# A causal mask as rows of the contraction, residues on GpSimd, and a new order of steps, in a hybrid block

## What is computed

```python
qkv = x @ qkv_w.T + qkv_b                      # 16 heads of width 8
q = q * cos + rotate_half(q) * sin;  k = k * cos + rotate_half(k) * sin
scores = einsum('bhsd,bhtd->bhst', q, k) / sqrt(8)
scores = where(key position > query position, finfo.min, scores)
out = softmax(scores) @ v,  then @ proj_w.T + proj_b
```

## Time and profile before

| | us |
|---|---|
| median of 3 runs | 749.57 |
| lowest and highest | 744.65 and 756.94 |
| the profiled execution | 753.01 |
| its span in the trace | 750.9 |

### The profile page before, as it was taken

The page is one execution under the profiler, slowest core; times in us unless marked ns, Lnnn a source line. Parts: engine busy times, 40 slices in busy tenths (PEclk is TensorE's granted clock), DMA queues, the critical chain, the costliest instruction groups (busy, mean ns, idle before and its releaser), DMA issues.

```text
span 750.9 us, 17433 instructions
## 1 busy us (share of the span) xinstructions
PE 653.8 (87%) x6640; PEld 375.3 (50%) x6670; DVE 563.3 (75%) x1571; ACT 426.4 (57%) x900; POOL 187.8 (25%) x231
## 2 busy tenths in 40 slices
...
PEclk9689896599999999999999999999999999999985
...
GB/s 107 1 1 1 16 69 101 2 17 2 87 100 1 17 98 89 2 10 66 113 17 24 52 99 29 2 58 76 55 9 56 63 64 17 96 75 3 16 1 14
DMA packets 20934, 32.37 MB, mean 43 GB/s; under 512 B 3178, under 2 KB 18282, under 8 KB 18538
## 3 DMA queue, kind: packets, MB, share of 16 engines
...
...
## 4 chain that ended last, share of the span: by engine, by line
PE 55%; DVE 24%; issue 8%; ACT 7%; DMA 3%; POOL 2%; SPq 1%; DVEq 0%; ACTq 0%; POOLq 0%
PE ps L1066 8%; PE ps L1021 8%; PE ps L1051 8%; DVE mrow L1491 7%; PE ps L795 5%; PE ps L869 3%; DVE qkf L1460 3%; PE ps L896 3%; PE ps L1053 3%; DVE am L1335 3%; PE ps L1023 2%; PE ps L790 2%; PE ps L916 2%; ACT pT L762 2%; PE ps L905 2%
## 5 line engine op out<-in xcount | busy, mean ns | idle before, releaser
L1491 DVE TENSOR_REDUCE mrow<-ps 128x1 f32<-128x384 f32 (+3 forms) x352 | 221.4, 634 | 78.5 <-PE ps L1023 76.0
L762 ACT ACTIVATE pT<-ps 128x512 f32<-128x512 f32 (+1 forms) x352 | 186.9, 558 | 105.1 <-PE ps L1053 101.6
L1021 PE MATMUL ps<-ks,qs 72*128 72x512 bf16 (+3 forms) x512 | 140.0, 309 | 17.3 <-DVE mrow L1491 14.1
L1051 PE MATMUL ps<-qs,ks 75*128 75x256 bf16 (+3 forms) x512 | 131.5, 305 | 4.1 <-DMA qs<-mT 2.5
L1023 PE MATMUL ps<-cbf 128*128 128x128 bf16 x512 | 101.5, 224 | 0.0
L1066 PE MATMUL ps<-pT,va 128*32 128x512 f32 (+3 forms) x1024 | 96.1, 451 | 5.3 <-ACT pT L762 5.0
L1021 PEld LDWEIGHTS ps<-ks,qs 72*128 72x128 bf16 x512 | 50.3, 99 | 96.0 <-DVE mrow L1491 78.2
L1053 PE MATMUL ps<-cbf 128*128 128x128 bf16 x512 | 98.0, 221 | 0.0
L546 POOL TENSOR_TENSOR spread<-state,cst 128x144 f32<-128x144 f32 x112 | 47.5, 445 | 186.8 <-DVE state L1364 153.2
L1051 PEld LDWEIGHTS ps<-qs,ks 75*128 75x128 bf16 x512 | 50.5, 99 | 76.0 <-ACT pT L762 30.6
L534 POOL TENSOR_TENSOR xe<-lpart,hot 96x1024 bf16<-96x1024 bf16 x32 | 60.3, 1893 | 47.8 <-DVE lpart L1321 47.8
...
## 6 DMA issues: line engine op xcount, KB each, us to landing
...
qs<-mT SPq DMA_DIRECT2D x48, 8.0 KB
```

The source lines that it names most:

```text
L762: act.activation(pT[:, c0:c0 + m, P_OFF[kt]:P_OFF[kt] + width], ps[:, score_banks(b)[n % len(score_banks(b))], 0:m * width].rearrange("p ( ...
L1021: pe.matmul(o, qs[0:K_MAX, f % RING, h, qt * P:(qt + 1) * P], ks[0:K_MAX, f % RING, h, 0:width], start=True, stop=False, skip_group_check= ...
L1051: pe.matmul(o, ks[0:K_ALL, place, h, kt * P:(kt + 1) * P], qs[0:K_ALL, place, h, kt * P:T], start=True, stop=False, skip_group_check=True)
L1491: dve.tensor_reduce(mrow[:, qt, h0:h0 + m], ps[:, max_banks(b)[n % len(max_banks(b))], 0:m * width].rearrange("p (m k) -> p m k", k=width) ...
```

## The change

Both mask matmuls go. Instead `qs` and `ks` get 43 more rows (`MARKS`, rows 75 to 117), written once: the row of a key and that of a query hold powers of two whose products add up to a large negative number exactly where the key is later than the query in its tile. They are built from the identity and a triangle by six DVE instructions on 43 columns, turned by two PE transposes, copied by ACT, and spread by six DMAs to the three places of the ring. Each product of scores is split: the diagonal tile takes 118 rows (`K_DIAG`), the rest of the width 72 rows (maxima) or 75 (attention). Where the tile is the whole width, there is one matmul. As rows 72 to 74 of `ks` hold ones, the same rows of `qs` must be zero during the maxima, so SP writes zeros there for each half batch (24 KB, one DMA more among those that `stacked` counts; PE's maxima wait for them).

In batches 1 to 6 (`residues_aside`) the four subtractions of the parts per batch move from DVE to GpSimd, behind its three `rsqrt` steps. All five order strings are written anew: DVE has 24 steps fewer for `m` and one more for `x`, GpSimd 24 more for `m`; PE, ACT and SP one more for `x` each, the setting up of the marks. The strings are left out here, and so are the declarations of semaphores.

```diff
-N_STACK = 16 * (len(Q_COPIES) + len(K_COPIES))
+N_STACK = 16 * (len(Q_COPIES) + len(K_COPIES) + 1)
+MARKS = (P + 2) // 3
+K_DIAG = K_ALL + MARKS
+MARK = (2.0 ** -39, 2.0 ** 12, 2.0 ** 63)
...
+        marks_tok = pT[:, 2, 0:MARKS].bitcast(BF16).rearrange("p (s r) -> p s r", s=2)
+        marks = pT[0:MARKS, 3, 0:T].bitcast(BF16).rearrange("p (s t) -> p s t", s=2)
...
-        ones_in = sem("ones_in")
+        ones_in = [sem("ones_in%d" % place) for place in range(RING)]
...
+        after = cst[:, C_AFTER:C_AFTER + P]
...
-        future_qk = cbf[:, P:2 * P]
...
+        def residues_aside(b):
+            return 0 < b < B - 1
...
         def va_heads(b):
...
+        zeros = consts_bf[0:1, 2 * P:3 * P].unsqueeze(1).broadcast_to([PARTS, HH * C, P])
...
-                sp.dma_start(ks[K_MAX:K_ALL, place, :, :], ones[:, 0:HH, :]).then_inc(ones_in, 16)
+                sp.dma_start(ks[K_MAX:K_ALL, place, :, :], ones[:, 0:HH, :]).then_inc(ones_in[place], 16)
             def norm(b):
...
+                    sp.dma_start(qs[K_MAX:K_ALL, f % RING, :, :].rearrange("p h (c t) -> p (h c) t", t=P), zeros
+                                 ).then_inc(stacked[f % RING], 16)
             def maxima(b):
+                if b == 0:
+                    yield
+                    sp.wait_ge(marks_ready, 1)
+                    for place in range(RING):
+                        for side, dst in enumerate((qs, ks)):
+                            sp.dma_start(dst[K_ALL:K_DIAG, place, :, :],
+                                         marks[:, side, :].unsqueeze(1).broadcast_to([MARKS, HH, T])
+                                         ).then_inc(marks_in[place], 16)
                 for f in (2 * b, 2 * b + 1):
...
+                for side in range(2 if residues_aside(b) else 0):
+                    yield
+                    pool.wait_ge(part0, b * 2 + side + 1)
+                    pool.tensor_tensor(rope1[:, side, :], qkf[:, side, :], parts[:, 0, side, :], ALU.subtract).then_inc(res1, 1)
+                for side in range(2 if residues_aside(b) else 0):
+                    yield
+                    pool.wait_ge(part1, b * 2 + side + 1)
+                    pool.tensor_tensor(parts[:, 2, side, :], rope1[:, side, :], parts[:, 1, side, :],
+                                       ALU.subtract).then_inc(part2, 1)
             def maxima(b):
...
             def maxima(b):
+                if b == 0:
+                    yield
+                    act.wait_ge(marks_ps, 1)
+                    act.activation(marks.rearrange("p s (c t) -> p s c t", c=C),
+                                   ps[0:MARKS, BK_MAX, :].bitcast(BF16)[:, 0:2 * P].rearrange("p (s t) -> p s t", s=2)
+                                   .unsqueeze(2).broadcast_to([MARKS, 2, C, P]), ACT.Copy).then_inc(marks_ready, 1)
                 for f in (2 * b, 2 * b + 1):
...
+                        if n == 0 and b == 0:
+                            for place in range(RING):
+                                act.wait_ge(marks_in[place], 32)
...
             def maxima(b):
...
+                if b == 0:
+                    yield
+                    pe.wait_ge(masks_in, 16)
+                    pe.wait_ge(marks_step, 6)
+                    for side in range(2):
+                        mm = pe.transpose(ps[0:MARKS, BK_MAX, :].bitcast(BF16)[:, side * P:(side + 1) * P],
+                                          marks_tok[:, side, :], ident_bf)
+                    mm.then_inc(marks_ps, 1)
                 for f in (2 * b, 2 * b + 1):
                     for n, (qt, h0, m) in enumerate(MAX_GROUPS):
...
-                                pe.wait_ge(masks_in, 16)
+                                pe.wait_ge(marks_ready, 1)
+                            if f < RING:
+                                pe.wait_ge(marks_in[f], 32)
+                                pe.wait_ge(ones_in[f], 16)
...
                         for h in range(h0, h0 + m):
...
-                            pe.matmul(o, qs[0:K_MAX, f % RING, h, qt * P:(qt + 1) * P], ks[0:K_MAX, f % RING, h, 0:width],
-                                      start=True, stop=False, skip_group_check=True)
-                            mm = pe.matmul(o[:, qt * P:(qt + 1) * P], ident_bf, future_qk,
-                                           start=False, stop=True, skip_group_check=True)
+                            own_tile = slice(qt * P, (qt + 1) * P)
+                            if qt > 0:
+                                pe.matmul(o[:, 0:qt * P], qs[0:K_MAX, f % RING, h, own_tile],
+                                          ks[0:K_MAX, f % RING, h, 0:qt * P], start=True, stop=True, skip_group_check=True)
+                            mm = pe.matmul(o[:, own_tile], qs[0:K_DIAG, f % RING, h, own_tile],
+                                           ks[0:K_DIAG, f % RING, h, own_tile], start=True, stop=True, skip_group_check=True)
...
                     for i in range(m):
...
-                        pe.matmul(o, ks[0:K_ALL, place, h, kt * P:(kt + 1) * P], qs[0:K_ALL, place, h, kt * P:T],
-                                  start=True, stop=False, skip_group_check=True)
-                        mm = pe.matmul(o[:, 0:P], ident_bf, future_kq, start=False, stop=True, skip_group_check=True)
+                        own_tile = slice(kt * P, (kt + 1) * P)
+                        mm = pe.matmul(o[:, 0:P], ks[0:K_DIAG, place, h, own_tile], qs[0:K_DIAG, place, h, own_tile],
+                                       start=True, stop=True, skip_group_check=True)
+                        if kt + 1 < C:
+                            mm = pe.matmul(o[:, P:width], ks[0:K_ALL, place, h, own_tile], qs[0:K_ALL, place, h, (kt + 1) * P:T],
+                                           start=True, stop=True, skip_group_check=True)
...
                 def values(g, kt):
...
-                if b == 0:
-                    pe.wait_ge(masks_in, 16)
-                    pe.wait_ge(ones_in, 16 * RING)
...
-                for side in range(2):
+                for side in range(0 if residues_aside(b) else 2):
...
-                for side in range(2):
+                for side in range(0 if residues_aside(b) else 2):
...
             def maxima(b):
+                if b == 0:
+                    yield
+                    dve.wait_ge(consts_in, 16)
+                    for k in range(3):
+                        n = len(range(k, P, 3))
+                        for side, (table, mark) in enumerate(((ident, -MARK[2 - k]), (after, MARK[k]))):
+                            to, columns = marks_tok[:, side, 0:n], table[:, k:P:3]
+                            if k == 0:
+                                ins = dve.tensor_scalar(to, columns, mark, None, ALU.mult)
+                            else:
+                                dve.wait_ge(marks_step, 2 * k)
+                                ins = dve.scalar_tensor_tensor(to, columns, mark, to, ALU.mult, ALU.add)
+                            ins.then_inc(marks_step, 1)
...
                 for f in (2 * b, 2 * b + 1):
                     for n, (qt, h0, m) in enumerate(MAX_GROUPS):
```

More of the change, by code:

```diff
@@ L86 @@
 PE_ORDER = (
[L87 to L96, removed]
@@ L97 @@
[L97 to L99 removed]
+    "ssssssssssmsssssssssssssssssssmsxssssssmmsssssmsmssssmsmssssssssssssssmssmssmsssmsssssssssssssmxssxsxxmx"
+    "sxxsxsxsxsxxsxsxsxsssxssxmxssxssxssxmxssxssxssxaassxaasaxsxaxssxsmaxamxssxsxsaaxmxaaasxaaxmxsxaamxsaxasx"
@@ new lines @@
+    "maxaaxasaaaasxaasssxaaxamaxsaxssaxaxaamaxaaxaasxaasaaxsasxasxaaaxasasxsaxaaamxaaxsaxmsxasxasxsxamsxasxax"
+    "ssxamxsaxaasxssxaaxssxasxaasaxaaxaaxsxaaxasxsxaaasxmaaxmxsxaxaasaaxsxaaxaaxaaaaxasaxamaasxsaaxmxssxaxasx"
+    "aaaaxasaxsxasaxasaxsasaxsxaaxaamxaaxsaxmassxsaxssxmxsaxsxasxsxsaxssxsxssxaxssxaaaxsxaamaxaaxsaasxaaxasax"
+    "saxaasamxasamxaaaasasaaaaxmaaaasxmaxasxsaxaaxasaaxaxasxsaxaaaxasxsxamxsaaxmaaaxsamxaaxaasxsaaxsxasxsasxs"
+    "axssmxsaxsxasxaxsssxasxaaxassxsxaasxsaxsaxaasxaasxaaxssaxaaaxaasxamaxaxaamaaxsaxasxaaaxaaaxasxaaaxasxaam"
@@ new lines @@
+    "xaaaxssxmxsxsaaxaxsaaxsaxasxaxaasaxaaxsamxaaxassaxmaxsaxsmaxssxasxassxmaxssxaxasxasxsxaasxaaxaassxaasxsx"
+    "aaxssxsaxaaaasaxsaxassaxaamsxamxsaxaaxaaaxaaaxsaxasxaaaxmasxaaaaxaxaaaxsxasxaaxmxaaxssaxaasxaaaxsaaxsaxm"
+    "axmassxsaxmsxasxassxasxaxasasxsxaxasxsxmxssxssxaaaaxssaaxssxaaxssxsaaaxaasasaaxssxaaxamaaxmaaxaaxaaaxaax"
+    "axaaxmaaxmxaaaxaaxaaaxaxaaxaxamaaxmxaaxaaxaaxamaxxaxaxaxmxaxxaxxaxaxaaxaaxaxaaxaaxaxaaxaxaaaxaxaaxaaaxaa"
+    "aaaxxaaaaxaxaxaxxxaaxxaaxxxaaaxaaaaaxaxaxxxaxaaaxaxaaaxaaaxxxaxaaxaxaxaxxxaaaaxxaxaxaxaaaxaxxaxaaxxaaaaa"
@@ L100 @@
+    "xaaaxaaaaaaaaaaaaaaaaaaaaaaaaaaaaaaaaaaaaaaaaaaaaaaaa"
 )
 ACT_ORDER = (
[L102 to L105, removed]
@@ new lines @@
+    "maasaaaamasaaaaaxasssaasaaaaasassaasmassasssaassasaaaasaasaamaaasamxsssssasnsmsaamaaamaamaasaaaasamaaaxa"
+    "aassasasaaamasssasaassasaaasaasassamsaamaaaasaaamaasasxsmssssamsanasasaamaaaaasaaaaaaamaaasaxaasasaaaaas"
```

(8 more changed lines are left out.)

27 lines of the change are left out of this document (16 added, 11 removed).

## The result

| | before | after |
|---|---|---|
| median, us | 749.8 | 794.79 |
| lowest and highest | 744.65 and 756.94 | 790.1 and 796.36 |
| profiled execution and its span | 753.01, 750.9 | 795.49, 793.7 |

The ratio is 1.061 [1.054, 1.069]: the change is slower, and my range ended at 741. (Ratios leave out runs over 1.5% above their kernel's fastest, medians are over all runs, and the two differ where a kernel scatters, as e5, e7 and e12 do.)

A forecast was written before the change was run, and what follows sets the result against it. PE's work was taken to set the middle's pace, DVE close behind. Masks 34 + residues 5.4 - collisions 2.5 - path 1.2 - zeros 0.5 - setup 1 = 34 us; four fifths, 27, off 749.6 gave 722 us, range 703 to 741.

The forecast's parts named there:

- The marks' transfers: Six spreads of marks on SP, 2.1 MB, would move while its queue is idle: cost 0, if late up to 18 us.
- 34 us of the masks lie on the chain: PE gives up 56 us net of splits; 61% of the masks lie on the chain, so 34 us net come off it.
- I take four fifths: Discount on the summed 34 us, as another chain shows when the longest shortens: 27 us of gain.
- the maxima don't gain: Rival, 17%: reductions and their one bank set the maxima's pace, so removing their masks brings nothing; gain 14 us, 736 us.
- A new order brings its own gain: Rival, 13%: redrawn order strings fill PE's waits, so all 34 us and 10 more come: 44 us, 705 us.
- PE busy down by more than 50 us: Sign expected in the changed profile: PE's busy time falls by over 50 us with the mask matmuls gone.
- The distance of 59 ns: On PE, 128-column matmuls start 59 ns apart, so 1024 masks cost 60 us; more contraction rows should cost nothing.
- Residues: +5.4, -2.5, -1.2: Chain effect of moving 24 subtractions to GpSimd: 5.4 us gained on DVE, 2.5 lost to collisions, 1.2 on the maxima's path.
- the 8 us: DVE time taken for collisions with the residues moved to GpSimd, between estimates of 6 and 31 us.
- Zeros 0.5, setting up 1: Chain costs: 0.5 us for 16 DMAs of zeros on SP, 1 us for preparing the marks in the first scan.
- The clock falls: Rival, 6%: less dense PE drops to 1.2 GHz for 80 us after 170 us: 767 us; for part of it, 740.
- GpSimd holds the scan: Rival, 4%: in batches 1 to 6 residues waiting for ACT delay `spread_state` and PE's `across`; at 8 us a batch, 771 us.

The follow-up runs named there:

- e5: The kernel before with its 1024 mask matmuls left out and nothing in their place, old order, residues on DVE: 758.92 us, ratio 0.996 to before.
- e7: The change with cut marks transfers (masks off, residues on GpSimd), but in the five order strings of the kernel before: 747.82 us, ratio 0.991 to before.
- e12: e1 with every score product whole over 72 or 75 rows and no mask, marks and zeros still transferred: 748.37 us, ratio 0.981 to before.
- e1: The changed kernel with each of the six marks transfers cut into 32, 8 and 3 rows: 725.49 us, ratio 0.970 to before.
- e4: The kernel before with marks (cut transfers) for its mask matmuls, residues on DVE, old order plus the marks' step: 751.65 us, ratio 1.002 to before.
- e9: The kernel before, mask matmuls kept, with residues on GpSimd and the five new order strings: 748.58 us, ratio 0.997 to before.
- e6: The kernel before, masks and order kept, with the residues of batches 1 to 6 on GpSimd: 753.44 us, ratio 1.003 to before.
- e3: e1 with the residues of batches 1 to 6 back on DVE: 755.6 us, ratio 1.005 to before.
- e8: e1 with each half batch's zeros sent in 24 packets of 1 KB instead of 96 small ones: 728.67 us, ratio 0.971 to before.
- e11: e9 with the mask matmuls left out and nothing in their place, so no marks, zeros or splits: 741.25 us, ratio 0.985 to before.
- e13: e12 with all score products over 118 rows, the marks being zeros: 726.28 us, ratio 0.968 to before.

## Why the prediction was wrong

**The marks' transfers, the step that failed.** "the marks are ready when PE has passed 29 steps of the first scan by its new order string, so they move while the queue is idle; cost 0". Three things in it were wrong. They were ready (ACT's copy of them ends at 56.2 us), but SyncE wasn't free to issue them: from 11.6 us on it stood at the load of `x` for batch 2 and waited for batch 1's `x` to be read, until 80.6 us. The trace of before has the same wait: there the load is issued at 78.8 us, in 0.40 us. The rate was taken from stacks of 72 rows and 9.83 us for 1.2 MB; 2.1 MB in rows of 43 took 6 x 14.8 = 89 us. And what stands behind them in SyncE's string, the spills, was priced at nothing: the bound "up to 18 us" is that of late marks alone. The hole is 69 us (after against e1).

**The sum without it.** 27 us forecast; e1 gains 750.91 - 725.49 = 25.4 us against the before timed with it, and 725 lies in my range. The size was right, several of its reasons were not:

- *34 us of the masks lie on the chain.* As a share of the present chain it was read rightly, as a gain it was not: in the old order the time doesn't fall (e4, and e5 without any mask), in part, by the estimate above, as the clock falls. "I take four fifths" can't stand for that: what the next chain is depends on the order, not on a fraction. The rival that the maxima don't gain (17%, 736 us) had the right mechanism for the old order, as waits for reductions grew by 20 us, but it still had 14 us of gain where e4 has none.
- *A new order brings its own gain (13%).* With the masks, it and the residues together bring 0.3% (e9), inside the noise; with less for PE to do it brings 22 us by the medians and 16 by the ratios (e7 to e1), most of e1's gain, as far as the steps that I placed by hand in e7 do it justice.
- *PE busy down by more than 50 us.* 653.8 to 610.4 in e1, 43 us; part of the rest may be the clock, as e1 has 13 us more at 1.2 GHz, the lower level. The distance of 59 ns held for 72 and for 118 rows alike, here in e1 (start, us):

```profile
317.59 0.23 PE L1083 MATMUL ps<-ks,qs 72*128 72x128 bf16 x1
317.65 0.22 PE L1085 MATMUL ps<-ks,qs 118*128 118x128 bf16 x1
```

- *Residues: +5.4, -2.5, -1.2.* On GpSimd one takes 1.16 us, less than the 1.34 I bounded it with. DVE is busy 548.0 us in e1: 563.3 less the 16.8 moved is 546.5, so collisions and the setting up together are 1.5 us there. But the other kernels with the residues on GpSimd are at 550.2 to 552.6 us in the new order, 4 to 6 us above 546.5, and at 555.4 (e6) and 555.9 (e7) in the old, 9 us above: so what collisions cost seems to depend on the order, and the 8 us fits the old one. That "the other batches have slack" was wrong: the landing is on the chain in three batches. Alone the move gives nothing (e6); with masks off and in the new order it decides (e3 to e1, 30 us by the medians, 27 by the ratios; e3's steps too were placed by hand).
- *Zeros 0.5, setting up 1.* Both too small to see: e8 shows nothing from the packets, e12, which has the marks and zeros transferred and unused, has the ratio 0.981 [0.974, 0.988] where e11 without them has 0.985 [0.981, 0.989], and e1's first read back is at 109.05 against 108.6.
- *The clock falls (6%).* Not the cause here, though the change has 81.0 us at 1.2 GHz from 170 us on, where before has 23.3: 47.6 of them lie before 620 us, where before has none, and the clock is 0.59 from 170 to 220 us, behind the stretch in which PE stood still. Without the hole, in e1, it is 36.4 us. But the mechanism is real, and e5, e11 and e12 show it: removing work cost clock. It hits the tail and the stretch before it, which I hadn't priced. The Trainium skill, "TensorE: Matmul & The Clock Gate", Part 1, has activity hold the clock up. The traces agree, with 76.4 us (e5) and 105.9 us (e11) at 1.2 GHz for 23.3 before; that e12 and e13, with the same columns, differ by 58 us is not explained by it.
- *GpSimd holds the scan (4%).* Not seen: no wait of `across` for it; the residues wait 25 us for ACT in all (18.4 for the first part, 6.5 for the second).

The best kernel of the study is e1, the change with its six transfers cut to 32, 8 and 3 rows: 725.49 us, 3.0% faster than before and 8.7% faster than the change.
